# A chunked scan: decays spread by transfers instead of by VectorE and TensorE, and GpSimd's two operations tied to other points of a chunk

## The reference

```python
dt = jnp.clip(jax.nn.softplus(dt + dt_bias[None, None, :]), 0.001, 0.1)
A = -jnp.exp(A_log)
dA = jnp.minimum(jnp.exp(dt * A[None, None, :]), 0.99)
def step(h, inp):
    x_t, B_t, C_t, dA_t = inp
    dBx = jnp.einsum('bhp,bn->bhpn', x_t, B_t)
    h = jnp.clip(dA_t[:, :, None, None] * h + dBx, -10.0, 10.0)
    y_t = jnp.einsum('bn,bhpn->bhp', C_t, h)
    return (h, y_t)
y = y + x_multi * Dparam[None, None, :, None]
```

## Time and profile before

| | us |
|---|---|
| median of 3 runs | 1819.15 |
| lowest and highest | 1818.82, 1821.85 |
| the profiled execution | 1810.79 |
| its span | 1808.7 |
| PE busy | 1701.5 (94%) |
| DVE busy | 1607.2 (89%) |
| ACT busy | 1476.5 (82%) |
| POOL busy | 653.6 (36%) |

### The profile page before, as it was taken

One profiled execution on the slowest core, in us unless ns is written; L12 is line 12 of the kernel. 1 busy time (PEld: TensorE's weight loads), 2 busy tenths in 40 slices (PEclk: granted clock), 3 DMA queues, 4 the chain that ended last, 5 costly groups with the idle time before them and its releaser, 6 DMA issues.

```text
span 1808.7 us, 40081 instructions
## 1 busy us (share of the span) xinstructions
PE 1701.5 (94%) x15396; PEld 658.2 (36%) x15396; DVE 1607.2 (89%) x2294; ACT 1476.5 (82%) x2806; POOL 653.6 (36%) x932
## 2 busy tenths in 40 slices
PE   6899999999999999999999999999999799899784
PEld 4432222222222222278622222222222345466553
DVE  7899999999999999945499999999997587699778
ACT  5679999999999999943399999999999567767455
POOL 1433310222444444100045565556501133133437
PEclk9999999999999999999999999999999999899798
DMA  4523222111221122278512211221102343422121
GB/s 127 175 71 85 87 65 69 57 58 35 71 61 56 57 67 66 73 209 228 143 51 64 55 45 52 59 63 47 41 10 58 90 134 97 138 65 63 42 63 47
DMA packets 152765, 142.15 MB, mean 79 GB/s; under 512 B 40394, under 2 KB 131533, under 8 KB 152418
## 3 DMA queue, kind: packets, MB, share of 16 engines
q1 hardware_dynamic: 144226, 122.37, 23.5%
q0 software_dynamic: 8352, 17.29, 3.3%
HBM read 76.60 MB, written 60.03 MB: 76 GB/s over the span
## 4 chain that ended last, share of the span: by engine, by line
PE 77%; DVE 10%; ACT 9%; issue 2%; POOL 1%; DMA 0%; POOLq 0%; DVEq 0%; ACTq 0%
PE PS L2027 30%; PE PS L2126 18%; PE PS L2011 11%; ACT probs L1347 6%; PE PS L2076 4%; PE PS L2061 2%; PE PS L2170 1%; PE PS L2176 1%; PE PS L2249 1%; DVE mxp L907 1%; DVE hst L1119 1%; PE PS L2053 1%; DVE VP L1094 1%; DVE MXV L1125 1%; PE PS L2331 1%
## 5 line engine op out<-in xcount | busy, mean ns | idle before, releaser
L907 DVE TENSOR_REDUCE mxp<-PS 128x1 f32<-128x1024 f32 x1024 | 1170.1, 1212 | 16.3 <-PE PS L2011 10.4
L1347 ACT ACTIVATE probs<-PS 128x512 f32<-128x512 f32 x2048 | 1096.3, 597 | 61.2 <-PE PS L2126 14.7
L2027 PE MATMUL PS<-probs,VH 128*32 128x256 f32 x8192 | 642.5, 391 | 1.8 <-ACT probs L1347 1.0
L2126 PE MATMUL PS<-stacks 51*128 51x512 bf16 x2048 | 438.5, 387 | 20.2 <-ACT probs L1347 16.4
L2011 PE MATMUL PS<-stacks 48*128 48x512 bf16 x2048 | 416.2, 380 | 2.2 <-DVE mxp L907 1.2
L2027 PEld LDWEIGHTS PS<-probs,VH 128*32 128x32 f32 x8192 | 173.1, 108 | 412.1 <-issue 229.7
L2126 PEld LDWEIGHTS PS<-stacks 51*128 51x128 bf16 x2048 | 115.0, 93 | 460.0 <-ACT probs L1347 421.5
L1713 POOL DMA_INDIRECT S<-oe_d,ROWI x128 | 130.0, 1015 | 130.0 <-PE PS L2027 124.1
L1683 POOL DMA_INDIRECT xe_d<-S,ROWI x128 | 125.4, 980 | 135.7 <-PE PS L2027 113.9
L1661 POOL CAST spl<-nmx 128x8 bf16<-128x8 f32 x64 | 12.7, 199 | 304.8 <-DVE nmx L863 226.6
L2011 PEld LDWEIGHTS PS<-stacks 48*128 48x128 bf16 x2048 | 106.0, 95 | 10.5 <-DVE mxp L907 5.8
(11 more groups left out here) (363 smaller groups left out, 1852.1 us busy)
## 6 DMA issues: line engine op xcount, KB each, us to landing
stacks<-qkl_d SPq DMA_DIRECT2D x128, 96.0 KB
xe_d<-zt SPq DMA_DIRECT2D x16, 640.0 KB
XNT<-xe_d SPq DMA_DIRECT2D x32, 320.0 KB, 3.8
oe_d<-XNT SPq DMA_DIRECT2D x32, 320.0 KB, 3.2
stacks<-qkl_d SPq DMA_DIRECT2D x128, 64.0 KB
o_d<-SG SPq DMA_DIRECT2D x256, 32.0 KB
ews<-in_ew_dram SPq DMA_DIRECT2D x33, 192.0 KB, 2.4
stacks<-qkl_d SPq DMA_DIRECT2D x128, 32.0 KB
```

The source lines that it names most:

```text
L907: v.tensor_reduce(mxp[:, n // 2, n % 2:n % 2 + 1], MXB[n % 2].rearrange("p a c -> p (a c)"), X_AX, ALU.max).then_inc(mx_done, 1)
L1347: act.activation(probs[:, at:at + 512], PS[:, bank_of(u, e), :], ACT.Exp, scale=float(1.0 / np.sqrt(np.float32(DK)))).then_inc(exp_done, 1)
L2027: mm = pe.matmul(OB[32 * jg:32 * jg + 32, c:c + 256], VH[w][:, kt, :], probs[:, at:at + 256], start=(kt < 2 and half == 0), stop=(kt >= TC ...
L2126: pe.matmul(PS[:, bank_of(u, e), :], KS[w][o:o + KROWS + 3, kt * P:(kt + 1) * P], QS[w][o:o + KROWS + 3, q0:q0 + 512], start=True, stop=Tr ...
```

## The change

The sums of log decays are made once for the whole sequence, by two matmuls behind the decays' last step (`decay_sums`): one has the sums as rows (16 x 4 x 2 chunks and heads by 128 steps), the other as columns. VectorE copies the first to `LR` and, negated, the second to `NL`. SP stores `LR` to DRAM (`rows_d`) and, for each chunk, loads its rows back, broadcast to 128 partitions (`LW`, 512 KB, two buffers) and to 64 and 64 partitions (`LE`, twice 128 KB, two buffers). VectorE's `decay_args` takes the place of `spread_decays` and of the mask: eight instructions of 128x128 subtract the column from the rows and cut what lies above the diagonal with a constant of -10000 (`PAST`). ScalarE takes the exponentials of these and of `LE`, and makes the bf16 copy by a second exponential. `chunk_sums` and the mask are gone.

On GpSimd, `scaled_x` of chunk c+1 now stands ahead of the addition of chunk c and waits for bd_set (VectorE's `BD` of its chunk). The addition of chunk c waits for hst_set (VectorE's `hst2` of chunk c) beside y_out.

```diff
+            def load_decays(c):
+                w = c % 2
+                hold(opb_ready, c - 1)
+                rows = rows_d.rearrange("(b c) n -> c b n", b=B)[c]
+                sp.dma_start(LW[w].rearrange("p (b h) t -> p b (h t)", b=B), rows.unsqueeze(0).broadcast_to([P, B, NH1 * P])).then_inc(lw_ld[w], 16)
+                for b in range(B):
+                    sp.dma_start(LE[w][rows_of(b), :], rows[b:b + 1, :].broadcast_to([DS, NH1 * P])).then_inc(le_ld[w], 16)
...
-                    load_chunk(0)
+                    load_b_c(0)
+                    hold(rows_out, ROWS_OUT + 1)
+                    sp.dma_start(rows_d.rearrange("t (h s) -> (t h) s", h=NH1), LR[:, :]).then_inc(rows_st, 16)
+                    load_b_x(0)
+                    hold(rows_st, ROWS_ST + 16)
+                    load_decays(0)
                     load_chunk(1)
+                    load_decays(1)
...
+            for c in range(2, 4):
+                load_chunk(c)
             for c in range(2, TCH):
-                load_chunk(c)
+                load_decays(c)
+                if c + 2 < TCH:
+                    load_chunk(c + 2)
...
-            def spread_decays(c):
-                after(v, la_ready, c)
-                link(v.tensor_copy(ldc[:, :, :].unsqueeze(2), ldt[:, :, c:c + 1, :]))
-                v.tensor_tensor(lb, TRI.unsqueeze(1).broadcast_to([P, B * NH1, P]),
-                                ldc.rearrange("p b h -> p (b h)").unsqueeze(2).broadcast_to([P, B * NH1, P]), ALU.mult).then_inc(lb_set, 1)
+            def decay_args(c):
+                w = c % 2
+                v.wait_ge(lw_ld[w], LW_BASE + 16 * (c // 2 + 1))
+                for b in range(B):
+                    for h in range(NH1):
+                        i, col = b * NH1 + h, (b * TCH + c) * NH1 + h
+                        ins = v.scalar_tensor_tensor(LW[w][:, i, :], LW[w][:, i, :], NL[:, col:col + 1], PAST, ALU.add, ALU.min)
+                ins.then_inc(args_set, 1)
 
             def chunk_operands(c):
                 w = c % 2
                 if c + 1 < TCH:
-                    spread_decays(c + 1)
+                    decay_args(c + 1)
                 v.wait_ge(d_done, c + 1)
-                v.tensor_tensor(DM, DE, TRI.unsqueeze(1).broadcast_to([P, B * NH1, P]), ALU.mult).then_inc(dm_done, 1)
...
             def chunk_exps(c):
                 w = c % 2
-                act.wait_ge(la_ready, c + 1)
+                act.wait_ge(args_set, c + 1)
                 after(act, ops_ready, c)
-                act.activation(DE, PS[:, 0:2, :].rearrange("p b (h t) -> p (b h) t", h=NH1), ACT.Exp).then_inc(d_done, 1)
+                act.activation(DM, LW[w], ACT.Exp).then_inc(d_done, 1)
...
-                act.wait_ge(dm_done, c + 1)
-                act.activation(DMb[w][:, :, 1:P], DM[:, :, 0:P - 1], ACT.Copy)
-                act.activation(DMb[w][:, :, 0:1], DM[:, :, P - 1:P], ACT.Copy).then_inc(opb_ready, 1)
+                act.activation(DMb[w][:, :, 1:P], LW[w][:, :, 0:P - 1], ACT.Exp)
+                act.activation(DMb[w][:, :, 0:1], LW[w][:, :, P - 1:P], ACT.Exp).then_inc(opb_ready, 1)
...
+            scaled_x(0)
             for c in range(TCH):
...
+                if c + 1 < TCH:
+                    scaled_x(c + 1)
                 pool.wait_ge(xd_made, XM_BASE + c + 1)
                 pool.wait_ge(y_out, c + 1)
+                pool.wait_ge(hst_set, HALVES + c + 1)
...
-            chunk_sums(0)
             router_logits()
...
             for c in range(TCH):
-                if c + 1 < TCH:
-                    chunk_sums(c + 1)
                 chunk_products(c)
```

More of the change, by code:

```diff
@@ L151, in build @@
         lda_d = dram("lda_d", (N, NH1))
+        rows_d = dram("rows_d", (NT, NH1 * P))
         y_d = dram("y_d", (N, DI))
@@ L249, in build @@
         sc_aff = sb("sc_aff", [P, 3, DI])
-        lb, DE, DM, MM0 = (VP[:, 8 * i:8 * i + 8, :] for i in range(4))
+        LW0, LW1, DM, MM0 = (VP[:, 8 * i:8 * i + 8, :] for i in range(4))
+        LW = [LW0, LW1]
         MM = [MM0, YM[:, 0:8, :]]
@@ L263, in build @@
         BD = [heads(t) for t in (probs[:, 3072:3584], ym_flat[:, 2048:2560])]
-        ldc = sb("ldc", [P, B, NH1])
+        LE = [wa[i].rearrange("p t c -> p (t c)") for i in range(2)]
+        NL = sb("NL", [P, NT * NH1])
+        LR = sb("LR", [P, P])
         HS = sb("HS", [P, NH1, HP])
@@ L353, in build @@
         tile_ld = [sem(f"tile_ld{i}") for i in range(4)]
[L354 to L355 removed]
+        dt_set, sums_ready, args_set, gg_set, d_done, el_done, opb_ready, vr_out, ops_ready, c_done, y_out, hs_done = (
+            sem(n) for n in ("dt_set", "sums_ready", "args_set", "gg_set", "d_done", "el_done", "opb_ready", "vr_out", "ops_ready", "c_done", "y_out", "hs_done"))
+        lw_ld, le_ld, LW_BASE = m_ld[0:2], m_ld[2:4], 64 * UNITS // 4
+        rows_out, ROWS_OUT = h_carried, 1
+        rows_st, ROWS_ST = xct_st, 16
         bnd_read, yc_ready = sem("bnd_read"), sem("yc_ready")
@@ L358, in build @@
         xd_made, XM_BASE = xc_ready, NB
+        bd_set, hst_set, HALVES = nmx_ready, spl_ready, 2 * UNITS
         okv = sb("okv", [P, 1])
@@ L1118, in chunk_state @@
             def chunk_state(c):
-                link(v.tensor_tensor(hst2[:, :, :], HS[:, :, :], E2[c % 2][:, :, P - 1:P].broadcast_to([P, NH1, HP]), ALU.mult))
+                v.tensor_tensor(hst2[:, :, :], HS[:, :, :], E2[c % 2][:, :, P - 1:P].broadcast_to([P, NH1, HP]), ALU.mult).then_inc(hst_set, 1)
+                v.wait_ge(hst_set, HALVES + c + 1)
                 v.wait_ge(y_out, c + 1)
@@ L1136, in _ @@
             router_scores()
+            decay_args(0)
             chunk_operands(0)
@@ L2217, in b_dt, with decay_sums @@
                 mm.then_inc(bd_ready, 1)
+            def decay_sums():
+                pe.wait_ge(dt_set, 1)
+                decays = DT.rearrange("p t h -> p (t h)")
+                pe.matmul(PS[:, 7, 0:P], decays, TRI, start=True, stop=True).then_inc(sums_ready, 1)
+                pe.matmul(PS[:, 1, 0:P], TRI, decays, start=True, stop=True).then_inc(sums_ready, 1)
             def router_in():
@@ L2294, in _ @@
             z_x_tile(j, 1)
+            decay_sums()
             router_in()
@@ L2306, in turned @@
                 pe.matmul(PS[:, 2, b * P:(b + 1) * P], BCT[c % 4][rows_of(b), 0:P], BCT[c % 4][rows_of(b), P:2 * P], start=True, stop=True).then_inc(gg_set, 1)
-            def chunk_sums(c):
-                pe.wait_ge(lb_set, c + 1)
-                after(pe, d_done, c)
-                scaled = lb.rearrange("p (b h) t -> p b (h t)", b=B)
-                for b in range(B):
-                    pe.matmul(PS[:, b, :], BELOW, scaled[:, b, :], start=True, stop=True)
-                after(pe, el_done, c)
-                for b in range(B):
-                    mm = pe.matmul(PS[rows_of(b), 7, :], onesq[:, 0:DS], scaled[:, b, :], start=True, stop=True)
-                mm.then_inc(la_ready, 1)
             def chunk_products(c):
@@ L2484, in layout @@
         "ident": np.eye(P, dtype=f),
-        "consts": np.concatenate([level, end, tri, np.repeat(np.eye(B), DS, axis=0), 1 - tri], axis=1).astype(f),
+        "consts": np.concatenate([level, end, tri, np.repeat(np.eye(B), DS, axis=0), -1e4 * (1 - tri)], axis=1).astype(f),
         "hz": states.astype(f),
```

42 lines of the change are left out of this document (26 added, 16 removed).

## The result

The change makes the kernel slower: 1930.9 us in the median of 4 runs (1930.24 to 1935.88) against 1818.99 of the kernel before on the same chip, a ratio of 1.0615 with a 95% interval of 1.059 to 1.0641. The forecast was 1898 us with a range of 1870 to 1930. The direction and the mechanism came as forecast. The size did not: the median lies just outside the range.

The account below looks back on a forecast made before the run. VectorE was taken as the bound. The start, 12 turns of 14.2 us and one chunk of 6.2 put chunk 13 79 us later: 1810.79 becomes 1890, plus 8.4 gives 1898 us, range 1870 to 1930.

Parts of the forecast that it names:

- The ring: Per-chunk cycle from L1119's end through GpSimd's addition, SP's issues, LW, decay_args and operands to the next L1119: 14.2 us.
- The landing: LW's time from SP's issue to arrival in each chunk: 4.4 us, with ends 2.8 and 6.1.
- `decay_args`: VectorE's eight new 128x128 instructions in each chunk: 0.2 us each, 1.6 in all.
- The upper neighbour: Upper bound for VectorE's eight new instructions, from L1212's mean of 338 ns: 2.7 us.
- The other links: Remaining terms of a chunk's cycle: addition 1.5, semaphore 0.1, six issues 3.5, operands 2.5, GpSimd overlap 0.2, L1119 0.4 us.
- The start: Scan's start, with new stores, waits and loads: L1119 of chunk 0 ends at 1594.4 instead of 1581.14, 13.3 us later.
- Chunk 13: One more chunk after the 12 turns, without the wait for LW: 6.2 us.
- I count nothing: TensorE's lost sums and ScalarE's changed work: neither was or becomes the bound, so no time counted.
- rival 2: TensorE falls to half clock, perhaps throughout; the last two chunks take some 8 us more: 1906 us, chance 0.25.
- Rival 3: A chunk's transfers crowd each other, LW landing after 6.1 us or later: 22 us more, 1920 us, chance 0.10.
- The placement: GpSimd's addition starting behind L1119 lets that VectorE instruction fall from 1.52 to about 0.4 us: 1.1 us a chunk.
- The 8.4 us: Amount by which the runs' median, 1819.15, lay above the profiled execution, added to 1890 us to give the forecast.

Follow-up runs that it names:

- e1: The changed kernel, but SP issues the loads of chunk c+1 instead of c+2 behind the decays of chunk c; 1846.06 us, ratio 1.017.
- e2: The changed kernel with GpSimd's two operations as before, without waits for bd_set and hst_set; 1882.24 us, ratio 1.0375.
- e3: The changed kernel with SP's same two waits, but the decays' three transfers ahead of the chunk's six loads; 1876.57 us, ratio 1.0331.
- e9: The kernel of e6 with LW halved to 256 KB from chunk 2 on, outputs differing; one execution, a turn of 14.5 us (whole time 9367 us).
- e6: The changed kernel without loading LE from chunk 2 on, earlier sums being reused; 1919.32 us, ratio 1.0569.
- e5: The kernel of e1 plus four 128x512 matmuls ahead of each chunk's products, their results unread; 1827.86 us, ratio 1.006.
- e4: The kernel before the change with only GpSimd's new placement and waits, no transfers of decays; 1804.89 us, ratio 0.9946.
- e7: The kernel of e5 with two filler matmuls instead of four, LW's buffer released sooner and the scan's start reordered; 1828.58 us, ratio 1.0065.
- e8: The kernel of e4 plus only the LE transfers from chunk 2 on, TensorE keeping half of chunk_sums; 1796.34 us, ratio 0.99.

## Why the prediction was wrong in size

- **The mechanism: right.** The ring through L1157, GpSimd's addition, SP's six issues, LW and `decay_args` is in the timeline link by link, and 12 chunks turn in it. e1 takes the ring away by the order on SP alone, e2 and e3 shorten it by one link each, all as expected in sign. The errors are terms of its sum.
- **The landing, forecast 4.4: wrong, the largest miss.** It was taken from a row of 256 KB for a transfer of 512 KB, since the row was "most like it in form". e9 shows 3.56 us for 256 KB and e6 5.31 for 512 KB, and LE's two transfers add 0.65: 6.1 in the mean of the 12 turns (5.75 to 6.65). Size should have chosen the row, and that was the upper end, X with 6.1. That this fits so closely is in part luck: LW by itself lands in 5.3. The miss is 1.7 us a turn, 20 us in all.
- **`decay_args`, forecast 1.6: 2.11.** The eight take 346 ns each in the group of the page, and the next instruction starts 2.11 us behind the first. The upper neighbour, L1212, was the like one, read by its busy time: 8.6 us over 32 is 0.27 each, 2.15 for eight, whereas its mean of 338 ns counts overlaps twice. 0.5 a turn, 6 us.

```profile
L1133 DVE SCALAR_TENSOR_TENSOR VP<-VP,NL,cst 128x128 f32<-128x128 f32 x128 | 35.0, 346 | 134.3 <-DMA VP<-rows_d 134.3
```

- **The other links: right, nearly.** Addition with its wait 1.45 (forecast 1.5); six issues 3.78 in the turn shown (3.5; some single issues take 1.3 to 1.4 us instead of 0.6); operands 2.46 (2.5); L1154 0.87 instead of 0.68 beside GpSimd's L1897 (0.2 forecast); L1157 0.41 (0.4). With 0.08 for the semaphore, 5.78 and 2.11 this makes the 16.28 of the turn shown; the mean is 16.65. Over 12 turns the ring gives 29 of the 40 us by which the profiled execution (1930.28) is over the forecast's 1890. The others are the start 5.0, the part ahead of the scan 5.1, chunk 13 3.8, behind it 1.6, and 4.4 back in the last stage.
- **The start, forecast 13.3: 18.3.** The stores of z and x and the wait behind them took 9.47 us (1576.87 to 1586.34), not 7.0 as before; LW and LE of chunk 1, issued right ahead of them, are the likely cause, but no run tests it. That is 2.5; LW(2)'s landing of 5.92 is 1.5 more, `decay_args` 0.5, and SP comes to these stores 0.5 later than forecast. The rows:

```profile
1576.87 0.58 SPq L705 DMA_DIRECT2D zs_d<-SG  x1
...
1586.34 0.50 SPq L667 DMA_DIRECT2D HH<-bt_d  x1
...
1604.19 0.41 DVE L1157 TENSOR_TENSOR hst<-HS,probs 128x256 f32<-128x256 f32 x1
```

- **Chunk 13, forecast 6.2: 10.03.** Without the wait for LW TensorE at half clock is the bound. The idle time in front of VectorE's L1149 names it, and L2372 has the 3.68 us of the earlier trace rows:

```profile
1806.10 3.68 PE L2372 MATMUL PS<-probs,YM 128*128 128x64 f32 x16
...
1812.25 1.29 DVE L1149 TENSOR_TENSOR VP<-VP,PS 128x512 f32<-128x512 f32 x2 [3.38 <-PE PS L2358]
```

- **"I count nothing" for TensorE's lost sums: nearly right for the changed kernel, wrong once the ring is open (e1).** In the ring half clock cost nothing, as rival 2 said (in the turn shown VectorE waits for LW only), and behind it 3.8 us in chunk 13 and at most 1.6 after that, less than the 8 that the rival had. Rival 2's state, half clock throughout, is what happened. Its reason, the 8 us of waiting in each chunk, does not carry alone: in e1 TensorE waits 0.46 us a chunk and stays at half clock all the same, and e5's filler brings full clock back. The Trainium skill (TensorE: Matmul & The Clock Gate, HAM oscillation) ties the cold tiles to waits for a DMA; this case's trace agrees for the changed kernel and for the fall at the start of e1 (idle from 1570 to 1580 us, clock 0.50), but not for e1's loop, where the clock stays down without such a wait.
- **Rival 3 (transfers crowd)** had the landing right, 6.1, at a chance of 0.10, and with 1920 a time that was still short, since it left `decay_args` and the start as they were. The rivals were added one by one; here a landing of 6.1, the half clock and `decay_args` near its upper neighbour came together, and the high end of the range took in only the first two.
- **The placement: right.** 1.1 us a chunk of VectorE's time, in e4 and in the changed kernel. What the prediction did not see is that with it TensorE becomes the bound at 8.09, so that of this 1.1 only about half arrives (8.1 instead of 8.6 in the mean). The chunk of 8.02 that it read as "what a chunk takes now" was one of the short ones.
- **The 8.4 us** by which the runs of before lay above their profiled execution did not recur: the median after is 0.6 us above its own. Without it the forecast would have been 1890, and further off: that term brought the number nearer by luck.
- **The edge of the range was passed by 0.9 us only**, and the 5.1 us ahead of the scan are more than that. Without them the number would have been inside, with the same errors in the ring.

The estimate from the Trainium skill (DMA: Bandwidth & Descriptors, Anatomy of one DMA), 3.2 us for LW by a fit for the GpSimd path, was further off than the row taken. Its fixed part of 2.0 us is near the 1.8 found here, but the part that goes with bytes is some three times what the page's rate gives: 3.5 us for 512 KB, 150 GB/s, for this broadcast on SP's queue.

## What to carry to other kernels

When a change puts a transfer on the queue behind loads that wait for the end of a chunk, walk from the released semaphore to the first user of that transfer and back: if the walk returns to the same semaphore, the sum of its links is the new period, and e1 shows that the order on the queue alone can open it. Choose a landing time from a row of the same size first and the same form second, and add what is issued right behind it. Removing matmuls from TensorE can slow those that stay (e1: 3.68 us instead of 2.00), so after such a change read the granted clock before anything else; and split a change of two parts in two, since here one half alone gains 0.5% and with a third of the other half it gains 1.0%.

## What was not expected of the hardware

- TensorE busy 94% of the time at a granted clock of 0.50 for 100 us and more (e1), and at 1.00 with four matmuls of 512 columns more in a chunk (e5). With two it went up and down in e7 (0.84, busy 96.59 of 100 us) and stayed at 1.00 in the stretch shown of e8 (busy 49.84 of 50). How the chip decides stays open.
- A transfer of 512 KB from 4 KB of DRAM, broadcast to 128 partitions, lands in 5.31 us, 256 KB from 2 KB in 3.56.
- SCALAR_TENSOR_TENSOR of 128x128 with both tensors in SBUF: one more every 0.26 us. In e2, where GpSimd's two operations ran beside them (from 1640.35 to 1642.88), eight took 3.54 us:

```profile
1641.06 3.54 DVE L1133 SCALAR_TENSOR_TENSOR VP<-VP,NL,cst 128x128 f32<-128x128 f32 x8 [7.08 <-DMA VP<-rows_d]
...
1640.35 1.26 POOL L1903 TENSOR_TENSOR stacks<-stacks,VH 128x512 f32<-128x512 f32 x1 [8.93 <-ACT stacks L1588]
1641.57 1.31 POOL L1896 TENSOR_TENSOR VH<-probs,sc_aff 128x512 f32<-128x512 f32 x1
```

The placement that the change gives GpSimd avoids this: in the changed kernel the eight take 2.19 us in every chunk of the ring.
